# An order of steps for each engine in place of one common order, in a fused RWKV, attention and mixture-of-experts layer

## The reference

```python
x = x + rwkv(layernorm(x))        # k = x Wk, r = v = x Wr; wkv recurrence over time; sigmoid(r) * y; Wo
x = x + ffn(layernorm(x))
# ffn(x): h = rmsnorm(x); q = h Wq + bq; kv = (h Wdown + bdown) Wup + bup
#   attention for each token over its 16 heads of 32 columns: softmax(q k / sqrt(32)) v; x = x + out Wo + bo
#   h2 = rmsnorm(x); gate = softmax(h2 Wg + bg) over 8 experts
#   return x + sum over e of gate_e * (h2 We_e)
```

## Time and profile before

| | |
|---|---|
| median of 3 runs | 3332.1 us (3330.17 to 3335.84) |
| the profiled execution | 3332.17 us, of which its span is 3330.3 us |
| PE busy | 2887.2 us, 87% of the span |
| DVE busy | 2476.6 us, 74% |
| ACT busy | 956.6 us, 29% |
| POOL busy | 686.1 us, 21% |
| mean granted clock of TensorE | 0.941 |
| chain that ended last | PE 62%, DVE 23%, issue 7%, SP's queue 5%, DMA 2% |

### The profile page before, as it was taken

How to read it: one execution, slowest core, us unless ns; L and a number is a source line. 1 busy time by engine, 2 the same in 40 slices (tenths; PEclk the granted TensorE clock), 3 DMA queues, 4 the chain that set the end, 5 groups by cost and what they waited for, 6 DMA issues and landing times.

```text
span 3330.3 us, 53600 instructions
## 1 busy us (share of the span) xinstructions
PE 2887.2 (87%) x18864; PEld 1791.2 (54%) x18864; DVE 2476.6 (74%) x4548; ACT 956.6 (29%) x1823; POOL 686.1 (21%) x745
## 2 busy tenths in 40 slices
PE   2359999998888989989998898999889998999889
PEld 2235555554555655555564555555555555555544
DVE  5797777778777768777777777768777777877753
ACT  2243232322332322322331332232233232232320
POOL 0111222212122212222221222221222221212210
PEclk9669999999999999999999999999999999999999
DMA  6011111101111101111111111111111110111110
GB/s 192 15 24 20 33 33 26 30 24 33 20 33 27 33 20 33 20 33 26 33 27 26 20 33 30 29 26 27 27 26 33 27 33 20 32 21 33 26 20 13
DMA packets 588333, 102.96 MB, mean 31 GB/s; under 512 B 556562, under 2 KB 556690, under 8 KB 588050
## 3 DMA queue, kind: packets, MB, share of 16 engines
q1 hardware_dynamic: 588068, 99.40, 16.4%
HBM read 48.49 MB, written 16.78 MB: 20 GB/s over the span
## 4 chain that ended last, share of the span: by engine, by line
PE 62%; DVE 23%; issue 7%; SPq 5%; DMA 2%; ACT 0%; POOL 0%; DVEq 0%; ACTq 0%; POOLq 0%
PE bank L1049 49%; PE bank L1201 6%; DVE mcol L954 4%; SPq L424 4%; DVE zz L865 3%; PE bank L1079 3%; DVE ks L943 3%; DVE wkv L839 2%; PE bank L1191 2%; DMA qs<-m 2%; DVE acc L1028 1%; DVE wkv L827 1%; PE bank L1165 1%; DVE ht L935 1%; DVE zz L832 1%
## 5 line engine op out<-in xcount | busy, mean ns | idle before, releaser
L1049 PE MATMUL bank<-w_e,h2t 128*128 128x512 f16 x6144 | 1479.4, 398 | 19.1 <-DVE acc L1028 19.1
L1049 PEld LDWEIGHTS bank<-w_e,h2t 128*128 128x128 f16 x6144 | 617.9, 103 | 757.5 <-issue 123.1
L1028 DVE SCALAR_TENSOR_TENSOR acc<-bank,gates,acc 128x512 f32<-128x512 f32 x512 | 373.6, 737 | 164.7 <-PE bank L1049 163.6
L1201 PEld LDWEIGHTS bank<-vp,pr 128*128 128x128 f32 x2048 | 263.9, 197 | 24.0 <-DVE hrow L970 3.9
L1201 PE MATMUL bank<-vp,pr 128*128 128x33 f32 x2048 | 259.7, 275 | 3.8 <-ACT pr L608 2.7
L608 ACT ACTIVATE pr<-bank,col 128x512 f32<-128x512 f32 x256 | 171.9, 685 | 316.1 <-PE bank L1191 315.7
L865 DVE RECIPROCAL zz<-zz 128x256 f32<-128x256 f32 x128 | 219.1, 1733 | 46.8 <-POOL zz L462 46.8
L1049 PE MATMUL bank<-w_o,xo 128*128 128x512 f16 x768 | 174.3, 384 | 58.8 <-DVE xo L799 58.8
L455 POOL TENSOR_TENSOR e<-wkv 128x512 f32<-128x512 f32 x64 | 72.1, 1127 | 645.6 <-DVE wkv L827 645.6
L1191 PE MATMUL bank<-qs,ks 106*128 106x128 f16 x1024 | 104.5, 236 | 113.9 <-DMA qs<-m 113.9
L1182 PE MATMUL bank<-ks,qs 104*128 104x128 f16 x1024 | 90.8, 231 | 125.7 <-DMA ks<-k 65.7
(11 more groups left out here) (177 smaller groups left out, 3918.1 us busy)
## 6 DMA issues: line engine op xcount, KB each, us to landing
qs<-qo SPq DMA_DIRECT2D x384, 64.0 KB, 3.0
...
ks<-k SPq DMA_DIRECT2D x128, 64.0 KB, 3.0
...
qs<-m SPq DMA_DIRECT2D x256, 2.0 KB, 1.7
...
```

The costliest lines, as they stand in the source:

```text
L1028: V.scalar_tensor_tensor(out=acc[:, s, :], in0=moe_bank[u % 2][:, :], scalar=gates[:, s, e:e + 1], in1=acc[:, s, :], op0=ALU.mult, op1=ALU ...
L1049: ins = nc.tensor.matmul(dst, left(a), right(b), start=(n == 0), stop=(n == last))
L1201: ins = nc.tensor.matmul(att_bank[ATT_BANK["PV", k]][:, n * (HD + 1):(n + 1) * (HD + 1)], pr[:, k % 2, n * P:(n + 1) * P], vp[:, 4 * k + n ...
```

## The change

PE, DVE, ACT, POOL and SP get a table each, and `pipeline` walks through the engine's own. The steps, what a step does, the semaphores, buffers and DMAs are unchanged. SP's list is in effect what it was. On PE one step moves. On ACT the gate's exponential and mix_turn change places, and mix_exp 1 moves behind att_scores 3. On POOL att_stats and moe_acc change places. On DVE many steps move. In POOL's and ACT's tables the moe steps stand only for the places of the weight splits.

```diff
-        def pipeline(eng, steps, split=None, between=None):
+        def pipeline(eng, order, steps, split=None, between=None):
...
-                for name, k in ORDER:
+                for name, k in order:
...
-    ("att_up", 0), ("mix_v", 0), ("mix_decay", 0), ("att_stack", 0), ("moe", 2), ("mix_exp", 0),
...
+PE_ORDER = [
...
+DVE_ORDER = [
+    ("att_stats", 0), ("moe_gate", 0), ("att_norm", 0), ("mix_turn", 0), ("att_turn", 0), ("att_rest", 0),
...
-            pipeline(pe, {"mix_turn": mix_turn, "mix_k": mix_k, "mix_v": mix_v, "mix_project": mix_project,
+            pipeline(pe, PE_ORDER, {"mix_turn": mix_turn, "mix_k": mix_k, "mix_v": mix_v, "mix_project": mix_project,
```

More of the change, by code:

```diff
@@ L127, in att_before @@
             return ATT_USES[m], True
-ORDER = [
-    ("moe_acc", 0), ("att_stats", 0), ("moe_gate", 0), ("mix_turn", 0), ("att_norm", 0), ("moe", 0),
-    ("moe", 1), ("att_turn", 0), ("att_rest", 0), ("mix_k", 0), ("att_latent", 0), ("att_q", 0),
-    ("att_up", 0), ("mix_v", 0), ("mix_decay", 0), ("att_stack", 0), ("moe", 2), ("mix_exp", 0),
[L136 to L145, removed]
@@ new lines @@
+PE_ORDER = [
+    ("mix_turn", 0), ("moe", 0), ("moe", 1), ("att_turn", 0), ("mix_k", 0), ("att_latent", 0), ("att_q", 0),
+    ("att_up", 0), ("mix_v", 0), ("moe", 2), ("moe", 3), ("moe", 4), ("att_max", 0), ("att_max", 1), ("moe", 5),
+    ("att_max", 2), ("att_max", 3), ("moe", 6), ("moe", 7), ("moe", 8), ("att_scores", 0), ("att_scores", 1),
+    ("att_probs", 0), ("att_scores", 2), ("att_probs", 1), ("att_scores", 3), ("moe", 9), ("att_probs", 2),
+    ("att_scores", 4), ("att_probs", 3), ("att_scores", 5), ("moe", 10), ("att_probs", 4), ("att_scores", 6),
+    ("att_probs", 5), ("att_scores", 7), ("moe", 11), ("att_probs", 6), ("att_probs", 7), ("moe", 12), ("moe", 13),
+    ("att_project", 0), ("moe", 14), ("moe", 15), ("att_turn2", 0), ("mix_project", 0), ("att_gate", 0),
+]
@@ new lines @@
+DVE_ORDER = [
+    ("att_stats", 0), ("moe_gate", 0), ("att_norm", 0), ("mix_turn", 0), ("att_turn", 0), ("att_rest", 0),
+    ("mix_decay", 0), ("att_latent", 0), ("att_up", 0), ("moe", 0), ("moe", 1), ("att_stack", 0), ("moe", 2),
+    ("mix_sum", 0), ("att_vt", 0), ("moe", 3), ("mix_rec", 0), ("moe", 4), ("att_max", 0), ("mix_rec", 1),
+    ("att_max", 1), ("att_max", 2), ("att_max", 3), ("att_m", 0), ("moe", 5), ("mix_scan", 0), ("mix_num", 0),
+    ("moe", 6), ("mix_gate", 0), ("moe", 7), ("mix_split", 0), ("mix_decay", 1), ("att_probs", 0), ("att_probs", 1),
+    ("moe", 8), ("moe", 9), ("mix_sum", 1), ("att_probs", 2), ("att_probs", 3), ("moe", 10), ("att_probs", 4),
+    ("mix_rec", 2), ("att_probs", 5), ("mix_rec", 3), ("moe", 11), ("att_probs", 6), ("att_probs", 7),
+    ("att_back", 0), ("mix_scan", 1), ("moe", 12), ("moe", 13), ("mix_num", 1), ("att_project", 0), ("mix_gate", 1),
+    ("att_norm2", 0), ("moe", 14), ("mix_split", 1), ("pre_stats", 0), ("moe", 15), ("att_turn2", 0), ("pre_norm", 0),
+    ("mix_project", 0),
+]
@@ new lines @@
+ACT_ORDER = [
+    ("mix_turn", 0), ("moe_gate", 0), ("moe", 0), ("moe", 1), ("att_turn", 0), ("mix_k", 0), ("att_latent", 0),
+    ("att_q", 0), ("att_up", 0), ("mix_v", 0), ("moe", 2), ("mix_exp", 0), ("moe", 3), ("moe", 4), ("moe", 5),
+    ("mix_num", 0), ("moe", 6), ("moe", 7), ("mix_split", 0), ("moe", 8), ("att_scores", 0), ("att_scores", 1),
+    ("att_scores", 2), ("moe", 9), ("att_scores", 3), ("mix_exp", 1), ("moe", 10), ("att_scores", 4),
+    ("att_scores", 5), ("att_scores", 6), ("att_scores", 7), ("moe", 11), ("moe", 12), ("att_back", 0), ("moe", 13),
+    ("mix_num", 1), ("moe", 14), ("att_square", 0), ("moe", 15), ("mix_split", 1), ("att_turn2", 0),
+]
@@ L146 @@
+POOL_ORDER = [
+    ("att_stats", 0), ("moe_acc", 0), ("att_rest", 0), ("att_q", 0), ("att_up", 0), ("mix_decay", 0), ("mix_sum", 0),
+    ("mix_decay", 1), ("mix_sum", 1), ("att_square", 0), ("moe", 15), ("pre_stats", 0),
+]
+SP_ORDER = [
+    ("mix_k", 0), ("att_up", 0), ("att_m", 0), ("pre_load", 0), ("moe_store", 0),
 ]
```

10 lines of the change are left out of this document (5 added, 5 removed).

## The result

The change takes 3224.21 us (median of 4 runs, 3223.73 to 3233.0), where the kernel before, on the same chip, takes 3332.09 us: the ratio is 0.9681, with a 95% interval of 0.9663 to 0.970. That is 107.9 us less, where 146 were forecast. 3224 lies inside the stated range of 3150 to 3250, but outside 3150 to 3220, which the prediction gives as the forecast's own. The profiled execution took 3224.1 us (span 3222.3); the mean granted clock rose from 0.941 to 0.959.

A forecast was written before the change was run, and what follows sets the result against it. PE sets the pace, held by waits for m, ks and DVE's score reduces. About 4.7 us in each of 30 iterations (141 us), plus smaller gains in two other tiles, make 146 us off 3332.17: 3186 us, range 3150 to 3250.

The forecast's parts named there:

- L: The moment in an attention tile when ks has landed and PE starts the maxima; later times count from it.
- the first rival: DVE becomes the tight chain from L to att_probs 0, gain halved: 75 to 90 us, about 3250; chance 0.25.
- What bounds the kernel now: PE sets the pace; it waits for m (113.9 us), ks (65.7) and DVE's score-bank reduces (59.7).
- A new wait: Between maxima and scores, PE waits 0.95 and 1.4 us for DVE's drains of moe units 5 and 6.
- From L to m: DVE reduces from L+0.4, SP starts the m DMAs at L+7.5, m arrives at L+13.9 instead of L+16.6.
- A lost cover: Without unit 8 behind the scores, PE idles 0.6 us for ACT; first probs product at L+16.5, gain 4.8 us.
- Whether it is kept: From the first probs product to att_project: DVE keeps up, att_project at L+37.5, the 4.8 us gain stays.
- slack of nothing: DVE ends att_probs 0 at L+21.1, just before PE wants it at L+21.2 for the second probs pair.
- Up to L: Before the maxima: DVE's ks copies start earlier, so L comes 0 to 1.0 us earlier, taken as 0.5.
- The h rows: att_norm before mix_turn and POOL's att_stats before moe_acc bring the h rows earlier: 0.05 us per tile.
- The clock: A slow stretch in unit 8 or later costs 0 to 1.3 us per tile, taken as 0.65; units 5 to 7 hidden.
- signs of being wrong: PE waits for hrow in the probs, clock 0.5 to 0.6 from unit 8 on, or ks wait grows over 0.5 us.

The follow-up runs named there:

- e2_pe_only: The kernel before, with one move on PE alone: moe unit 8 ahead of att_scores 0 and 1; 3283.51 us.
- e3_dve_only: The kernel before, with DVE's new order alone, PE, ACT, POOL and SP keeping the common order; 3279.57 us.
- e1: The changed kernel with one swap undone: on POOL, moe_acc stands ahead of att_stats again; 3221.01 us.
- e10: The change with DVE's drains retimed and ACT's att_scores 0 and 1 ahead of mix_split 0, att_scores 4 ahead of mix_exp 1; POOL's moe_acc behind att_stats; 3189.96 us.

## Why the prediction was right, and where its size was off

The mechanism was right from L to att_project, and the number lies in the stated range. But it lies 4 us outside the forecast's own 3150 to 3220, in the part that was added for the first rival, and that rival's reason, DVE's chain from L to att_probs 0 stretched by itself, did not come; the lock of DVE and GpSimd that it names did stretch DVE, but in the gate, ahead of L. So the range held by its width, not because the whole sum was right.

- *What bounds the kernel now* was right: the waits for m and for the maxima, 173.6 us together, are what the change took away, and the largest of what came in their place are the two waits of *A new wait*.
- *From L to m* was right to 0.1 us: first reduce at L+0.43 (forecast L+0.4), SP's m DMAs at L+7.40 (L+7.5).
- *A new wait* too: 0.75 and 1.44 us (0.95 and 1.4), the scores at L+15.12 (L+15.1).
- *A lost cover*: the first probs product at L+16.29 (L+16.5), after 0.56 us of idling (0.6). e2_pe_only shows that this move of one unit alone gives about half of the gain, e3_dve_only that DVE's order alone gives as much.
- *Whether it is kept*: att_project at L+37.7 in the 16 tiles without a slow unit or group (forecast L+37.5); att_probs 0 is through on DVE at L+21.2 (L+21.1; the terms that are given add up to L+21.3). The slack of nothing held in these tiles. In the 10 tiles with slow maxima the reduces start later, PE's scores follow 1.2 us later, and att_project at L+38.9: there what delays DVE does move PE, though not quite one for one, and its cause is PE's clock, not DVE.
- *Up to L* was wrong: 0.5 us in a tile was taken, 15 us in the sum, and nothing came. The copies start 3.62 us after SP's first q DMA (forecast 3.72), 2.2 us earlier than before, but SP takes 13.05 us for the same DMAs, and L lies 15.68 us behind the start of the V products in the mean of 30 tiles, in the change as before. The 12.09 us of the last tile came from something else than the place of the copies (rows below). The rule that the prediction quoted and did not follow (Trainium skill, SBUF — State Buffer, "SBUF: two separate sides": compute and DMA do not slow one another) would have taken these 15 us off; the trace agrees with it.
- *The h rows*, put at a gain of 0.05 us in a tile, were a loss. Only the order of POOL's two steps was looked at, not what DVE does while POOL adds. The distance from att_project to the V products grew from 38.03 us (1507.06 to 1545.09) to 39.05 (1453.55 to 1492.60), and so by 17.1 us in the 17 tiles without a jump, nearly all of it by POOL's move, as e1 and e10 show. The 12 tiles at the loop's jump lost 5.7 us more, of which 4.3 are a slower moe unit 0, and the first of the 30 tiles 2.1.
- *The clock* was taken at 0.65 us in a tile for a slow unit 8 or later, and it cost 0.57, which is luck. Slow units 19 us behind L were in only 4 tiles (5.7 us of the path). The other 11.5 us come from 10 tiles with slow maxima and a slow unit 5 behind the wait for ks, a place that the prediction called hidden.

The trace of the kernel before already held a row against the reading of the last tile. These are SP and DVE in the second attention tile, which has mix beside it:

```profile
265.32 5.67 SPq L413 DMA_DIRECT2D qs<-qo  x8
...
274.57 2.81 SPq L417 DMA_DIRECT2D ks<-k  x4
```

```profile
271.20 4.45 DVE L943 COPY ks<-k 32x1024 f16<-32x1024 f16 x8
```

The copies start 5.88 us after SP's first DMA, as late as in other tiles, and yet SP took 12.06 us for its sixteen. So neither the place of the copies nor the absence of mix is needed for the short time; what is, no run here shows.

So the sum had 141 us for the 30 iterations, and 104.5 came: 15 less from *Up to L*, 26 less between att_project and the V products, and 5 more from L to att_project. The rest of the kernel gave 3.4 us where 5 were put.

Two of the three signs of being wrong appeared. The clock fell to 0.53 in unit 9. And the wait for ks grew by more than 0.5 us: from 1.84 to 2.51 in the tiles shown, from 65.7 to 88.7 us in the list. The prediction let it grow by the 0.53 us that PE no longer waits for the drain of unit 2, and shrink by the 0.5 us of *Up to L*; only the first came. PE's wait for hrow in the probs did not come, but for one of 0.8 us ahead of the 30 iterations. The period was forecast at 91.3 us in a tile without a jump; it is 93.86 in the tile shown (1453.55 to 1547.41) and 92.6 in tiles with no slow unit.
